# Gathered rows written to memory in one piece per half, statistics included

## The chip, the core and the metric

The kernel runs on one core of one Trainium2 chip. The metric is the device time of one execution in microseconds (us), read as the median of several runs.

## The reference

The input is x of shape (2, 2048, 128): two batches of 2048 tokens with 128 features. It goes through three residual blocks:

```python
x = x + 0.5 * ffn(layernorm(x))
x = x + attention(layernorm(x))
x = x + 0.5 * ffn(layernorm(x))
```

The feed-forward block is a mixture of four experts, of which each token uses one:

```python
idx = argmax(softmax(x @ Wg + bg))
h = gelu(x @ W1[e] + b1[e])          # 128 -> 512
y = h @ W2[e] + b2[e]                # 512 -> 128
out = sum over e of y[e] * onehot(idx)[e]
```

The attention is linear: 32 features elu(.)+1 per token for query and key, a sum k'v over the whole batch, and a normalisation of each token.

## The kernel before

**Tokens are sorted by expert.** A phase is one feed-forward block on one batch; there are four, in the order block one of batch 0, of batch 1, block two of batch 0, of batch 1. Before a phase, the router finds each token's expert and the place of the token in an order sorted by expert, and makes from it a table of row numbers, `src` (written by DVE in `route_src`). In a phase GpSimd (POOL) issues 16 indirect DMAs, `gather`, each of which fetches 128 rows in that order from a tensor in HBM into a tile G. Such a row has `RW` = 144 floats: the 128 features, then the mean, the reciprocal of the deviation (`rstd`), the token's own number and padding, so that whatever is known of the token travels with it. The tensors are `rows0` for the first block and `rows1` for the second, one for each batch.

**The visits.** A phase is worked off in V = 19 visits v, 16 tiles plus three borders between experts. For a visit, DVE normalises the gathered tile (`norm`, xn from G), TensorE (PE) turns it over (`turn_in`), ACT copies it to `hT_in`, PE multiplies by W1 (`up`), ACT applies Gelu, PE multiplies by W2 (`down`), and DVE adds the result to the tile in place (`finish`). PE does `up` three visits ahead of `down`. The weights of a visit with their biases are a slab, which SP copies within SBUF from the tile W1 five visits ahead (`copy_slab`). The sequence of each engine's instructions is written out by hand, in loops over v; semaphores alone tie the engines together.

**The front.** Before the first visit SP loads x of batch 0 in four pieces (`load_x`, into X0_0) and of batch 1 in two (X0_1), then W1 and b2. DVE computes bn_stats on each row of x, and the mean into `MR0`; POOL computes rstd (`pow_front`, a power, one instruction for each half of a batch); PE turns x over and multiplies by the gate weights, with ACT copying between the two (`front_copy`); DVE then routes. PE runs products of no use (`busy`) where it would otherwise wait, the longest being 24 of them ahead of tile 0.

**How rows0 is written before.** Features and statistics go apart. SP stores the features of a half as 8 strips of 512 bytes a partition (`store_x`), as soon as x has landed: for batch 0 ahead of the four loads of W2, for batch 1 at v = 2 and 4 of the first phase. The statistics, strips of 64 bytes, come from `MR0` (`store_stats`): ACT issues them for batch 0, and SP for batch 1 at v = 7 and 8. The first gather of a batch waits for all four stores (64 counts), as well as for `src`.

**What follows from program order.** A wait on SP holds up the slab copies behind it; a wait on ACT holds up the `front_copy` of the next group; a wait on POOL holds up all later gathers. POOL starts with two `pow_front`, a small product `place_tiles`, then eight gathers, then one for each visit, with the two `pow_front` of batch 1 at v = 3 and 4.

Of the kernel before, what the change touches and what calls it, by code (L numbers as in the profile page):

```python
# [16 lines left out]
def need(eng, stage, j):  # L17
    if j >= 0:
        eng.wait_ge(stage.sem, j + 1)
# [15 lines left out]
def build(nc, x, wq, wk, wv, proj, w1, b1, w2, b2, wg, bg, out):  # L35
    f32, bf16, i32 = mybir.dt.float32, mybir.dt.bfloat16, mybir.dt.int32
    ALU, ACT, AX = mybir.AluOpType, mybir.ActivationFunctionType, mybir.AxisListType

    P = 128
    B, L, D = x.shape  # L40
    NE, _, F = w1.shape
    R = proj.shape[1]
    NC = F // P
    T = L // P
# [5 lines left out]
    RW = D + 16  # L50
# [5 lines left out]
    XN = (4, 2)  # L56
# [7 lines left out]
    rows0_v = [r.rearrange("(p t) c -> p t c", t=T) for r in rows0]  # L64
    rows1_v = [r.rearrange("(p t) c -> p t c", t=T) for r in rows1]

    with ExitStack() as ctx:
        def sb(name, shape, dt=f32):
            return ctx.enter_context(nc.sbuf_tensor(name, shape, dt))

        def several(name, shape, n, dt=f32):
            return [sb(f"{name}{i}", shape, dt) for i in range(n)]

        def sem(name):
            return ctx.enter_context(nc.semaphore(name))

        def stages(prefix, names):
            return {n: Stage(sem(f"s_{prefix}_{n}")) for n in names.split()}
# [32 lines left out]
        same = sb("same", [P, P])  # L111
        warm, rest = sb("warm", [P, 1]), sb("rest", [P, 4 * P])

        X0 = several("X0_", [P, T, D], B)
        ST0 = several("ST0_", [P, T, 6], B)
        MR0 = several("MR0_", [P, T, RW - D], B)
        VE0 = several("VE0_", [P, T], B)
        ra, rb_, rc, rd, re = (sb(n, [P, T]) for n in ("ra", "rb", "rc", "rd", "re"))

# [52 lines left out]
        s_x = [[sem(f"s_x{b}_{i}") for i in range(XN[b])] for b in range(B)]  # L172
        s_rows0 = [sem(f"s_rows0_{b}") for b in range(B)]
        s_rows1 = [sem(f"s_rows1_{b}") for b in range(B)]
        s_const, s_constd, s_same = sem("s_const"), sem("s_constd"), sem("s_same")
        s_fold, s_foldd, s_warm, s_av, s_mean = sem("s_fold"), sem("s_foldd"), sem("s_warm"), sem("s_av"), sem("s_mean")
        s_slab = [sem(f"s_slab{k}") for k in range(NSLAB)]
        s_gather = [[sem(f"s_gather{b}_{t}") for t in range(T)] for b in range(B)]
        s_scatter, s_issued = sem("s_scatter"), sem("s_issued")
        s_dve = sem("s_dve")  # L180
        ln0 = stages("ln0", "ve rstd")
# [9 lines left out]
        def ph_of(f, b):  # L191
            return 2 * f + b
# [88 lines left out]
                return {10: range(4, 7), 11: (7,), 13: (8, 9)}.get(v, ())  # L281
            return range(v - NE, T) if v == V - 1 else (v - NE,) if v >= NE else ()

        def store_stats(eng, b, h):
            lo, hi = h * T // 2, (h + 1) * T // 2
            need(eng, ln0["rstd"], 2 * b + h)
            eng.dma_start(rows0_v[b][:, lo:hi, D:RW], MR0[b][:, lo:hi, :]).then_inc(s_rows0[b], 16)


        @block.sync  # L290
        def _(eng):
            H = T // 2
            w1_v = W1[:, :].rearrange("p (e k) -> p e k", e=NE)
            w2_v = W2[:, :].rearrange("p (c e d) -> p e c d", e=NE, d=D)

            def load_x(b, i):
                n = T // XN[b]
                eng.dma_start(X0[b][:, i * n:(i + 1) * n, :], x_b[b][:, i * n:(i + 1) * n, :]).then_inc(s_x[b][i], 16)

            def load_w2(e):  # L300
                eng.dma_start(w2_v[:, e, :, :], w2[e, :, :].rearrange("(c p) d -> p c d", p=P)).then_inc(s_w["w2"], 16)

            def store_x(b, h):
                for i in range(h * XN[b] // 2, (h + 1) * XN[b] // 2):
                    eng.wait_ge(s_x[b][i], 16)
                eng.dma_start(rows0_v[b][:, h * H:(h + 1) * H, 0:D], X0[b][:, h * H:(h + 1) * H, :]).then_inc(s_rows0[b], 16)

            for i in range(XN[0]):
                load_x(0, i)
            load_x(1, 0)  # L310
            load_x(1, 1)
            eng.dma_start(w1_v[:, :, 0:F], w1.rearrange("e d f -> d e f")).then_inc(s_w["w1"], 16)
            eng.dma_start(w1_v[:, :, F + NC:SW], b2.unsqueeze(0).to_broadcast([P, NE, D])).then_inc(s_w["b2"], 16)
            store_x(0, 0)
            store_x(0, 1)
            for e in range(NE):
                load_w2(e)

            def store_rows1(b, g):
                need(eng, lb["x2"], b * NG + g)  # L320
                need(eng, lb["rstd"], b * NG + g)
                need(eng, rt["src"], b)
                eng.dma_start(rows1_v[b][:, g * GS:(g + 1) * GS, :].rearrange("p t c -> p (t c)"),
                              G0[b][:, g * GS * RW:(g + 1) * GS * RW]).then_inc(s_rows1[b], 16)

            offs = {}

            def copy_slab(s):
                ph, v = divmod(s, V)
                if v % CHUNK == (s == 1):  # L330
                    need(eng, rt["visit"], ph)
                    v -= v % CHUNK
                    offs.update({ph * V + v + i: e for i, e in enumerate(loaded(eng, v_slab, ph, v, SW))})
                k = s % NSLAB
                need(eng, ffn["hT"], s - NSLAB)
                need_res(eng, s - NSLAB)
                eng.dma_start(slab[k][:, :], W1[:, bass.ds(offs[s], SW)]).then_inc(s_slab[k], 16)

            eng.wait_ge(s_w["w1"], 16)
            eng.wait_ge(s_w["b2"], 16)  # L340
            eng.wait_ge(s_foldd, 4)

            eng.dma_start(slab[0][:, :], W1[:, 0:SW]).then_inc(s_slab[0], 16)
            for s in range(1, SLAB_LEAD):
                if s > 1:
                    need(eng, ffn["norm"], s - 1)
                copy_slab(s)
            for s in range(2 * B * V):
                ph, v = divmod(s, V)
                if s + SLAB_LEAD < 2 * B * V:  # L350
                    copy_slab(s + SLAB_LEAD)
                if ph == 0 and v in (2, 4):
                    store_x(1, v // 2 - 1)
                if ph == 0 and v in (7, 8):
                    store_stats(eng, 1, v - 7)
                if ph in (1, 2) and 6 <= v < 6 + NG:
                    store_rows1(ph - 1, v - 6)

# [2 lines left out]
        def _(eng):  # L361
# [7 lines left out]
            for b in range(B):  # L369
                eng.memset(MR0[b][:, :, :], 0.0).then_inc(s_const, 1)  # L370
            eng.wait_ge(s_const, 7)
            for b in range(B):
                eng.iota(MR0[b][:, :, 2].bitcast(i32), pattern=[[1, T]], base=b * L, channel_multiplier=T).then_inc(s_const, 1)
            eng.affine_select(out=blocks[:, :], in_=blocks[:, :], compare_op=ALU.is_ge, fill=0.0, base=0,
# [18 lines left out]
            def pow_front(b, h):  # L393
                lo, hi = h * T // 2, (h + 1) * T // 2
                need(eng, ln0["ve"], 2 * b + h)
                ln0["rstd"].done(eng.tensor_tensor(MR0[b][:, lo:hi, 1], VE0[b][:, lo:hi], neghalf[:, lo:hi], ALU.pow))  # L396

# [20 lines left out]
            def gather(f, b, t, second=False, columns=4 * P):  # L418

                if second:  # L420
                    next(count)
                else:
                    rested(columns)
                if t == 0:
                    need(eng, rt["src"], ph_of(f, b))
                    if f == 0:
                        eng.wait_ge(s_rows0[b], 64)
                    else:
                        eng.wait_ge(s_rows1[b], 16 * NG)
                eng.indirect_dma_start(out=row(f, b, t, 0, RW), out_offset=None, in_=(rows0, rows1)[f][b],  # L430
                                       in_offset=bass.IndirectOffsetOnAxis(ap=src[f][b][:, t:t + 1], axis=0),
                                       engine_sem=issued.sem)\
                   .then_inc(s_gather[b][t], 16)
# [98 lines left out]
        def _(eng):  # L532
# [17 lines left out]
            def front_stats(b, lo, hi):  # L550
                eng.wait_ge(s_x[b][lo * XN[b] // T], 16)
                for t in range(lo, hi):
                    did(eng.bn_stats(ST0[b][:, t, :], X0[b][:, t, :]), t == hi - 1)

# [340 lines left out]
        def _(eng):  # L895
# [4 lines left out]
            def front_turn(k):  # L900
# [3 lines left out]
                for i in range(GS):  # L904
                    n = eng.transpose(U[k % 2][:, i * P:(i + 1) * P], X0[b][:, g * GS + i, :], ident[:, :])
                fr["xT"].done(n)
# [213 lines left out]
        def _(eng):  # L1120
# [10 lines left out]
            def front_copy(k):  # L1131
                need(eng, fr["xT"], k)
                need(eng, fr["mm"], k - 2)
                fr["xTs"].done(eng.activation(xTs[k % 2][:, :], U[k % 2][:, :], ACT.Copy))

            def copy_in(ph, j):
                first, n = GROUPS[j]
                need(eng, ffn["xT"], group(ph, j))
                ffn["xTs"].done(eng.activation(hT_in[ph % 2][:, first * P:(first + n) * P], TR[:, 0:n * P], ACT.Copy))  # L1139
# [47 lines left out]

            for k in range(NG):
                front_copy(k)
            front_copy(NG)  # L1190
            front_copy(NG + 1)
            store_stats(eng, 0, 0)
            store_stats(eng, 0, 1)
            hots(0, NG - 1)
            place_lanes(0)
            front_copy(NG + 2)
# [8 lines left out]
            for s in range(2 * B * V):  # L1205
                ph, v = divmod(s, V)
# [54 lines left out]
```

## Time and profile before

| | |
|---|---|
| median of 3 runs (lowest to highest) | 236.23 us (235.95 to 236.77) |
| profiled execution: time, span | 237.53 us, 235.8 us |
| PE busy | 207.2 us (88%) |
| DVE busy | 159.4 us (68%) |
| ACT busy | 126.9 us (54%) |
| POOL busy | 160.2 us (68%) |
| mean granted clock of TensorE | 0.969 |

The span is the time from the first to the last instruction on the core; the profiled execution's own time has 1.73 us around it. The busy time of PE contains the filler products. An engine's idle time counts only where something that ends the kernel waits for it, so the stages have to be read one by one.

### The profile page before, as it was taken

How to read it: one execution, taken by the hardware profiler on the slowest of the kernel's cores; microseconds unless marked ns; L12 is line 12 of the kernel's file. 1: busy time of each engine (PE TensorE's matmuls, PEld its weight loads, DVE VectorE, ACT ScalarE, POOL GpSimd, SP SyncE). 2: the span in 40 equal slices, each digit the busy share in tenths (PEclk: the TensorE clock that was granted, in tenths of full speed). 3: DMA queues.
4: the chain of work that ended last, by engine and by line, in shares of the span. 5: the costliest groups of instructions: out<-in, count | busy, mean ns of one | idle time of the engine just before them, and what ended most of it. 6: DMA issues, size and time to landing. Idle time of an engine off the chain costs nothing. (4 is left out here: it accounts for less than half of the span.)

```text
span 235.8 us, 6375 instructions
## 1 busy us (share of the span) xinstructions
PE 207.2 (88%) x1786; PEld 195.7 (83%) x1786; DVE 159.4 (68%) x641; ACT 126.9 (54%) x406; POOL 160.2 (68%) x225
## 2 busy tenths in 40 slices
PE   8989996996997999999969998999959899999900
PEld 7879996896997988889969897779959899999900
DVE  3699463579688989698887879788776545553400
ACT  1415055567554586635675676825565567765500
POOL 7221888882728687147138888756878888788775
PEclk9999999998899999999999999999979999999985
DMA  4999259982534462326703852517721976662111
GB/s 103 372 321 254 96 199 351 314 212 83 185 110 167 154 215 69 130 106 237 277 0 116 300 206 83 165 61 281 269 79 42 329 274 222 222 221 103 45 56 45
DMA packets 28454, 41.69 MB, mean 177 GB/s; under 512 B 7795, under 2 KB 14851, under 8 KB 28422
## 3 DMA queue, kind: packets, MB, share of 16 engines
q1 hardware_dynamic: 22368, 34.11, 40.5%
q0 software_dynamic: 3072, 6.82, 11.1%
q10 hardware_dynamic: 2982, 0.36, 1.0%
q8 instruction: 16, 0.26, 0.5%
q14 instruction: 16, 0.13, 0.2%
HBM read 9.41 MB, written 6.82 MB: 69 GB/s over the span
## 5 line engine op out<-in xcount | busy, mean ns | idle before, releaser
L1145 ACT ACTIVATE hT<-U,slab 128x128 f32<-128x128 f32 x304 | 86.7, 370 | 56.4 <-PE U L966 56.3
L966 PE MATMUL U<-hT_in,slab 128*128 (+1 forms) x608 | 82.8, 280 | 1.5 <-ACT hT_in L1139 1.3
L977 PE MATMUL DN<-W,hT 128*128 (+1 forms) x608 | 83.7, 282 | 0.2 <-issue 0.2
L966 PEld LDWEIGHTS U<-hT_in,slab 128*128 128x128 f32 x608 | 74.8, 194 | 2.7 <-issue 2.4
L977 PEld LDWEIGHTS DN<-W,hT 128*128 128x128 f32 x608 | 75.4, 195 | 1.4 <-issue 1.2
L430 POOL DMA_INDIRECT G<-rows,src x64 | 62.5, 977 | 15.2 <-issue 10.2
L729 DVE SCALAR_TENSOR_TENSOR G<-DN,mask,G 128x128 f32 (+1 forms) x76 | 26.4, 348 | 27.3 <-PE DN L977 24.6
L416 POOL MEMSET rest<- 128x512 f32 (+1 forms) x78 | 35.4, 454 | 6.3 <-DVE G L729 0.7
L442 POOL DMA_INDIRECT out_dram<-G x32 | 31.6, 988 | 7.3 <-issue 6.3
L705 DVE TENSOR_SCALAR xn<-G 128x128 f32<-128x128 f32 x64 | 23.7, 389 | 9.3 <-DMA G<-rows,src 9.0
L717 DVE SCALAR_TENSOR_TENSOR G<-slab,mask,G 128x128 f32 (+1 forms) x60 | 21.2, 353 | 6.7 <-DVE G L729 4.0
L1139 ACT ACTIVATE hT_in<-TR 128x128 f32<-128x128 f32 (+1 forms) x44 | 14.4, 327 | 17.8 <-PE TR L957 17.4
L957 PE MATMUL TR<-ident,xn 128*128 128x128 f32 x64 | 14.6, 280 | 7.5 <-DVE xn L705 6.3
L401 POOL TENSOR_TENSOR RS<-VE,neghalf 128x4 f32<-128x4 f32 x8 | 8.5, 1062 | 12.9 <-DVE VE L741 12.8
L406 POOL TENSOR_TENSOR G<-VE,neghalf 128x4 f32<-128x4 f32 x8 | 8.3, 1043 | 12.8 <-DVE VE L799 12.6
L957 PEld LDWEIGHTS TR<-ident,xn 128*128 128x128 f32 x64 | 8.3, 142 | 8.8 <-DVE xn L705 7.2
L898 PE MATMUL DN<-mean_w 128*128 128x128 f32 x104 | 14.6, 300 | 1.1 <-POOL mean_w L362 1.1
L898 PEld LDWEIGHTS DN<-mean_w 128*128 128x128 f32 x104 | 13.9, 215 | 1.1 <-POOL mean_w L362 1.1
L467 POOL TENSOR_TENSOR AV<-A,lane_f 128x256 bf16<-128x256 bf16 x4 | 3.3, 828 | 12.5 <-DVE A L651 6.9
L396 POOL TENSOR_TENSOR MR<-VE,neghalf 128x8 f32<-128x8 f32 x4 | 6.7, 1679 | 5.7 <-DVE VE L564 5.2
L734 DVE BATCH_NORM_STATS2 ST<-G 128x6 f32<-128x128 f32 x32 | 8.8, 287 | 1.6 <-issue 1.4
L656 DVE TENSOR_TENSOR SL<-slot_i,lane_b 128x512 bf16<-128x512 int32 x12 | 8.8, 784 | 0.0
(159 smaller groups left out, 219.7 us busy)
## 6 DMA issues: line engine op xcount, KB each, us to landing
slab<-W SPq DMA_DIRECT2D x76, 322.0 KB, 3.1
rows<-G SPq DMA_DIRECT2D x8, 288.0 KB, 2.1
rows<-X SPq DMA_DIRECT2D x4, 512.0 KB, 9.5
X<-in_L_attn_x_dram SPq DMA_DIRECT2D x4, 256.0 KB, 6.7
X<-in_L_attn_x_dram SPq DMA_DIRECT2D x2, 512.0 KB, 8.8
W<-in_L_ffn_W_dram SPq DMA_DIRECT2D x1, 1024.0 KB, 11.5
W<-in_L_ffn_W_dram SPq DMA_DIRECT2D x4, 256.0 KB, 6.0
G<-rows,src POOLq DMA_INDIRECT x64, 3.2
```

The costliest lines, as they stand in the source:

```text
L416: eng.memset(rest[:, 0:columns], 0.0)
L430: eng.indirect_dma_start(out=row(f, b, t, 0, RW), out_offset=None, in_=(rows0, rows1)[f][b], in_offset=bass.IndirectOffsetOnAxis(ap=src[f] ...
L442: eng.indirect_dma_start(out=out_rows, out_offset=bass.IndirectOffsetOnAxis(ap=index, axis=0), in_=row(1, b, t), in_offset=None, engine_se ...
L705: ffn["norm"].done(eng.tensor_scalar(xn[k % NXN][:, :], row(f, b, t), row(f, b, t, D, 1), row(f, b, t, D + 1, 1), ALU.subtract, ALU.mult))
L717: ffn["res"].done(eng.scalar_tensor_tensor(out=r, in0=slab[s % NSLAB][:, F + NC:SW], scalar=mask[f][b][:, v:v + 1], in1=r, op0=ALU.mult, o ...
L729: ffn["out"].done(eng.scalar_tensor_tensor(out=r, in0=DN[s % 2][:, 0:D], scalar=mask[f][b][:, v:v + 1], in1=r, op0=ALU.mult, op1=ALU.add))
L898: eng.matmul(DN[0][:, 0:P], mean_w[:, :], mean_w[:, :], start=True, stop=True)
L957: last = eng.transpose(TR[:, i * P:(i + 1) * P], xn[k % NXN][:, :], ident[:, :])
L966: i = eng.matmul(U[s % 3][:, c * P:(c + 1) * P], slab[s % NSLAB][:, c * P:(c + 1) * P], hT_in[ph % 2][:, bass.ds(v * P - expert_at[s], P)] ...
L977: i = eng.matmul(DN[s % 2][:, 0:D], hT[s % NHT][:, c * P:(c + 1) * P], W2[:, bass.ds(expert_at[s] + c * NE * D, D)], start=(c == 0 and not ...
L1139: ffn["xTs"].done(eng.activation(hT_in[ph % 2][:, first * P:(first + n) * P], TR[:, 0:n * P], ACT.Copy))
L1145: i = eng.activation(hT[s % NHT][:, c * P:(c + 1) * P], U[s % 3][:, c * P:(c + 1) * P], ACT.Gelu, bias=slab[s % NSLAB][:, F + c:F + c + 1])
```

## The change

A tile `XR` of 16 rows of 144 floats a partition takes the place of the statistics' tile, for each batch; the statistics are its last 16 columns. Batch 1 is loaded straight into the first 128 columns of `XR1`. Batch 0 is still loaded into a tile of its own, and ACT copies it to `XR0` in four instructions, behind `front_copy(3)`. One DMA a half then stores features and statistics together, 4608 contiguous bytes a partition on both sides. In batch 0 it waits for the copies and for rstd; the second half goes between the second and third load of W2. In batch 1 the stores stand at v = 5 and 6. ACT issues none. The first gather of a batch waits for two stores (32 counts).

```diff
-        X0 = several("X0_", [P, T, D], B)
+        XR = several("XR", [P, T, RW], B)
+        X0 = [sb("X0", [P, T, D])[:, :, :], XR[1][:, :, 0:D]]
...
-        MR0 = several("MR0_", [P, T, RW - D], B)
+        MR0 = [r[:, :, D:RW] for r in XR]
...
+            def store_rows0(b, h):
+                need(eng, ln0["rstd"], 2 * b + h)
+                if b == 0:
+                    eng.wait_ge(s_copied, (h + 1) * XN[0] // 2)
+                else:
+                    eng.wait_ge(s_x[b][h], 16)
+                eng.dma_start(rows0_v[b][:, h * H:(h + 1) * H, :].rearrange("p t c -> p (t c)"),
+                              XR[b][:, h * H:(h + 1) * H, :].rearrange("p t c -> p (t c)")).then_inc(s_rows0[b], 16)
...
-            store_x(0, 0)
-            store_x(0, 1)
-            for e in range(NE):
-                load_w2(e)
+            store_rows0(0, 0)
+            load_w2(0)
+            load_w2(1)
+            store_rows0(0, 1)
+            load_w2(2)
+            load_w2(3)
...
-                if ph == 0 and v in (2, 4):
-                    store_x(1, v // 2 - 1)
-                if ph == 0 and v in (7, 8):
-                    store_stats(eng, 1, v - 7)
+                if ph == 0 and v in (5, 6):
+                    store_rows0(1, v - 5)
...
-                        eng.wait_ge(s_rows0[b], 64)
+                        eng.wait_ge(s_rows0[b], 32)
...
+            def copy_rows(i):
+                lo, hi = i * T // XN[0], (i + 1) * T // XN[0]
+                eng.wait_ge(s_x[0][i], 16)
+                eng.activation(XR[0][:, lo:hi, 0:D], X0[0][:, lo:hi, :], ACT.Copy).then_inc(s_copied, 1)
...
             for k in range(NG):
                 front_copy(k)
+            for i in range(XN[0]):
+                copy_rows(i)
             front_copy(NG)
             front_copy(NG + 1)
-            store_stats(eng, 0, 0)
-            store_stats(eng, 0, 1)
```

On SP's queue, at the start of the program, these stood before (output and input of each DMA, and the semaphores it waits for; s_x0 and s_x1 tell of the landing of x, and W is W1 or W2 by its shape, 128x4x512 being W1 and 128x4x128 either b2 or W2):

```order
L298 DMA X_0<-in_L_attn_x_dram 128x512 x4
L298 DMA X_1<-in_L_attn_x_dram 128x1024 x2
L312 DMA W<-in_L_ffn_W_dram 128x4x512
L313 DMA W<-in_L_ffn_b_dram 128x4x128
L306 DMA rows_0<-X_0 128x8x128 [waits s_x0_1,s_x0_0]
L306 DMA rows_0<-X_0 128x8x128 [waits s_x0_3,s_x0_2]
L301 DMA W<-in_L_ffn_W_dram 128x4x128 x4
```

And these stand there now:

```order
L297 DMA X<-in_L_attn_x_dram 128x512 x4
L297 DMA XR<-in_L_attn_x_dram 128x8x128 x2
L315 DMA W<-in_L_ffn_W_dram 128x4x512
L316 DMA W<-in_L_ffn_b_dram 128x4x128
L308 DMA rows_0<-XR 128x1152 [waits s_copied,s_ln0_rstd]
L300 DMA W<-in_L_ffn_W_dram 128x4x128 x2
L308 DMA rows_0<-XR 128x1152 [waits s_copied,s_ln0_rstd]
L300 DMA W<-in_L_ffn_W_dram 128x4x128 x2
```

The stores have become one run of 1152 floats a partition, wait for more, and are apart; the load of batch 1 has become eight runs of 128 floats a partition, where it was one of 1024.

On SP's queue, in the first phase, this stretch stood before (ISA sets the address of a slab copy; the TENSOR_LOAD reads the table of visits). It begins with the second store of features of batch 1, at v = 4, and ends with the store of statistics at v = 7:

```order
L306 DMA rows_1<-X_1 128x8x128 [waits s_x1_1]
L337 ISA [waits s_ffn_res,s_ffn_hT]
L337 DMA slab<-W 128x644
L337 ISA [waits s_ffn_res,s_ffn_hT]
L337 DMA slab<-W 128x644
L264 TENSOR_LOAD v_slab_0 [waits s_rt_visit]
L337 ISA [waits s_ffn_res,s_ffn_hT]
L337 DMA slab<-W 128x644
L287 DMA rows_1<-MR_1 128x8x16 [waits s_ln0_rstd]
```

Now the two slab copies of v = 4 and 5 stand ahead of the first store of batch 1, and one more between the stores:

```order
L342 ISA [waits s_ffn_res,s_ffn_hT]
L342 DMA slab<-W 128x644
L342 ISA [waits s_ffn_res,s_ffn_hT]
L342 DMA slab<-W 128x644
L308 DMA rows_1<-XR 128x1152 [waits s_x1_0,s_ln0_rstd]
L342 ISA [waits s_ffn_res,s_ffn_hT]
L342 DMA slab<-W 128x644
L308 DMA rows_1<-XR 128x1152 [waits s_x1_1,s_ln0_rstd]
```

What was stored at v = 2 and 4 has moved behind the slab copy of v = 5, and each store there now waits for POOL's rstd.

## Rows read from the trace of the kernel before

**Rows 1.** The page of the profiled execution: DMA busy tenths in 40 slices of 5.9 us:

```profile
DMA  4999259982534462326703852517721976662111
```

**Rows 2.** Busy time by stage: stretch, its length, each engine, PEclk, DMA share, GB/s:

```profile
23.00:41.00 18.00, 16.20 (x140) 15.67 (x139) 8.47 (x40) 6.91 (x26) 14.78 (x20) 1.00 0.63 209
51.00:62.00 11.00, 8.88 (x74) 8.16 (x73) 10.17 (x42) 6.31 (x21) 5.49 (x8) 0.84 0.47 144
62.00:75.00 13.00, 12.34 (x111) 12.14 (x109) 9.52 (x39) 7.79 (x27) 7.39 (x11) 1.00 0.45 155
186.00:224.00 38.00, 38.00 (x341) 38.00 (x342) 17.74 (x55) 25.26 (x90) 31.50 (x45) 1.00 0.56 194
```

**Rows 3.** Timeline of PE: start, us, engine, line, tiles, idle before:

```profile
23.25 5.55 PE L898 MATMUL DN<-mean_w 128*128 128x128 f32 x48
41.51 0.44 PE L957 MATMUL TR<-ident,xn 128*128 128x128 f32 x2 [2.25 <-DVE xn L705]
56.34 0.44 PE L957 MATMUL TR<-ident,xn 128*128 128x128 f32 x2 [1.91 <-DVE xn L705]
```

**Rows 4.** Timeline of DVE:

```profile
22.33 0.18 DVE L691 TENSOR_SCALAR src<-tok 128x16 int32<-128x16 f32 x1
41.04 0.42 DVE L705 TENSOR_SCALAR xn<-G 128x128 f32<-128x128 f32 x1 [2.48 <-DMA G<-rows,src]
49.19 0.35 DVE L705 TENSOR_SCALAR xn<-G 128x128 f32<-128x128 f32 x1 [0.75 <-DMA G<-rows,src]
60.86 0.17 DVE L691 TENSOR_SCALAR src<-tok 128x16 int32<-128x16 f32 x1
```

**Rows 5.** Timeline of POOL:

```profile
12.35 1.65 POOL L396 TENSOR_TENSOR MR<-VE,neghalf 128x8 f32<-128x8 f32 x1 [0.93 <-DVE VE L564]
24.10 1.20 POOL L430 DMA_INDIRECT G<-rows,src  x1 [4.30 <-DMA rows<-MR]
42.95 1.70 POOL L396 TENSOR_TENSOR MR<-VE,neghalf 128x8 f32<-128x8 f32 x1 [0.45 <-DVE G L729]
44.84 1.01 POOL L430 DMA_INDIRECT G<-rows,src  x1 [0.18 <-issue]
61.32 1.04 POOL L430 DMA_INDIRECT G<-rows,src  x1 [0.55 <-DVE src L691]
```

**Rows 6.** Landings, from issue: b2 (L313); gathers (L430) from 24 and 36 us; statistics (L287):

```profile
L313 SPq DMA_DIRECT2D W<-in_L_ffn_b_dram x1: 947/947/947, 4.3 to 4.3; - x1
DMA to landing us min/median/max: 11.6/11.6/11.6
...
DMA to landing us min/median/max: 2.8/3.3/3.5
...
L430 POOL DMA_INDIRECT G<-rows,src x4: 950/950/977, 36.4 to 41.5; - x4
DMA to landing us min/median/max: 4.0/4.9/5.3
...
L287 ACTq DMA_DIRECT2D rows<-MR x2: 395/510/624, 15.6 to 16.1; - x2
DMA to landing us min/median/max: 4.9/6.0/7.2
```

**Rows 7.** SP's DMA queue: timeline of the loads of W2; instructions of L306 from 34 us:

```profile
13.23 5.26 SPq L301 DMA_DIRECT2D W<-in_L_ffn_W_dram  x4
...
L306 SPq DMA_DIRECT2D rows<-X x2: 601/760/920, 35.8 to 39.6; - x2
```

**Rows 8.** DMA in 8 to 11, 15 to 18 and 19 to 22 us:

```profile
DMA packets 693, 1.21 MB, mean 402 GB/s; under 512 B 186, under 2 KB 358, under 8 KB 693
...
DMA packets 1760, 0.86 MB, mean 286 GB/s; under 512 B 112, under 2 KB 1759, under 8 KB 1759
...
q10 hardware_dynamic: 1409, 0.09, 32.2%
```

**Rows 9.** Timeline of ACT:

```profile
15.19 0.60 ACT L1134 ACTIVATE xTs<-U 128x512 f32<-128x512 f32 x1 [3.49 <-PE U L905]
```

More of the change, by code:

```diff
@@ L176, in build @@
         s_fold, s_foldd, s_warm, s_av, s_mean = sem("s_fold"), sem("s_foldd"), sem("s_warm"), sem("s_av"), sem("s_mean")
+        s_copied = sem("s_copied")
         s_slab = [sem(f"s_slab{k}") for k in range(NSLAB)]
@@ L282, in stats_of @@
             return range(v - NE, T) if v == V - 1 else (v - NE,) if v >= NE else ()
[L284 to L287, printed above, removed]
         @block.sync
@@ L301, in load_w2 @@
                 eng.dma_start(w2_v[:, e, :, :], w2[e, :, :].rearrange("(c p) d -> p c d", p=P)).then_inc(s_w["w2"], 16)
[L303 to L306, printed above, removed]
+            def store_rows0(b, h):
[6 more added lines that the diff above has]
+                              XR[b][:, h * H:(h + 1) * H, :].rearrange("p t c -> p (t c)")).then_inc(s_rows0[b], 16)
             for i in range(XN[0]):
```

## The prediction, made before the changed kernel ran

> **What bounds the kernel now.** I read the page's slices of DMA activity first: the queues are full in the front (up to about 24 us) and again around 36 to 46 us, and the change acts in just these two places [rows 1]. Then the busy times by stage: late in the kernel PE has no idle time (38.00 of 38.00 us), so there nothing but its own work counts, while in 23 to 41 us it lacks 1.8 of 18, and in 51 to 62 us it is DVE that is full, 10.17 of 11 [rows 2]. The timelines say what those gaps are. PE waits 2.25 us ahead of 41.51 for xn, and DVE, which makes xn, waits 2.48 us until 41.04 for a gather [rows 3, 4]. DVE waits again, 0.75 us, ahead of 49.19, and from there it works through the router of the next phase without a stop, so that PE waits 1.91 us for it ahead of 56.34 [rows 3, 4]. Third, POOL: its first gather starts at 24.10, and was released by the statistics' store, though `src` was ready at 22.33 + 0.18 = 22.51 [rows 4, 5]. The last statistics were issued at 16.1 and took 7.2 us to land, at 23.3 [rows 6].
>
> The lateness of the first gather is not yet a lateness of the kernel. PE's filler runs from 23.25 to 28.80, and covers tile 0 [rows 3]. The gathers follow each other at POOL's own pace, though, so an early start helps whichever tile PE first has to wait for, and that is tile 7, whose gather was issued at 36.4 [rows 6].
>
> **The change part by part.**
>
> *The load of batch 1* is now in strips of 512 bytes. The mean rate in 8 to 11 us, large strips, is 402 GB/s; in 15 to 18 us, nearly all strips of 512 bytes, it is 286 [rows 8]. 1.05 MB take 2.6 us at the one and 3.7 at the other: 1.1 us more, in front of W1 and b2 on the same queue. The Trainium skill's page "DMA: Bandwidth & Descriptors", in its section "Specifications", puts the least transfer for full rate at 512 bytes; by that the 1.1 us would be nothing. The two rates above disagree with it here, and I go by them.
>
> *The stores of batch 0.* Before, 1.05 MB at 286 GB/s, 3.7 us, plus 64-byte strips: in 19 to 22 us 1409 packets of ACT's queue, most of the 2048, took 32.2% of three us, so some 1.4 us in all [rows 8]. Now 1.18 MB in strips of 4608 bytes, at 402 GB/s 2.9 us. That is 2.2 us less traffic against 1.1 more. When is the second half in? b2 was issued at 4.3 and landed 11.6 us later, at 15.9 [rows 6]; with the slower load 17.0. Behind it are the first half (0.59 MB, 1.5 us), two loads of W2 (0.52 MB at 286, 1.8 us) and the second half, 1.5 us: 21.8. The issue is no limit: rstd of half 1 is ready at 12.35 + 1.65 = 14.0 [rows 5]. ACT is idle from 15.19 - 3.49 = 11.70 on, waiting for PE, and four copies at the price of its copy of the same size at 15.19, 0.60 each, end at 14.1, hidden with 1.1 to spare [rows 9]. At 0.87 each they would still be. SP was ready for W2 at 13.23 before [rows 7], and now issues the first half at about 12.9, so the queue, full until 17, does not run dry. DVE's and POOL's work on the statistics keeps its count; only the stride of its elements changes, at no cost that I can see.
>
> *The first gather* then waits for `src` at 22.51, and not for the rows. Its start: a gather released by `src` later on starts 61.32 - (60.86 + 0.17) = 0.29 us behind it, while the first one started 24.10 - 23.3 = 0.8 behind the rows' landing [rows 4, 5]. So between 22.80 and 23.3, a gain of 0.8 to 1.3 us; I take 1.2, since the rows' wait is passed before `src` comes, as in the later gather.
>
> *The stores of batch 1* leave v = 2 and 4 (issued at 35.8 and 39.6 [rows 7]). Gathers up to 36 us landed in 2.8 to 3.5 us; the four from 36.4 to 41.5, beside those stores, in 4.0 to 5.3 [rows 6]. Gather 7 now starts at 36.4 - 1.2 = 35.2; with 3.5 us it has landed at 38.7, and its xn, 0.3 to 0.4 us of DVE, is ready at about 39.1. PE was free at 41.51 - 2.25 = 39.26. The whole 2.25 us goes.
>
> *What is late next.* POOL loses its 0.45 us of idle time ahead of 42.95, so its power of batch 1 comes 1.2 + 0.45 less 0.1, about 1.55 us earlier, and gather 11 starts at 44.84 - 1.55 = 43.3 [rows 5]. The first store of batch 1 is released by that same power, at 44.65 - 1.55 = 43.1, so it moves next to gather 11. With 3.4 us (as undisturbed) xn of tile 11 begins at 46.7, with 4.3 us (the disturbed end being 4.0 to 5.3) at 47.6; DVE is free for it at 49.19 - 0.75 - 2.25 = 46.2. Before it was 49.19: a lead of 1.6 to 2.5. The store (0.59 MB) occupies the queues for 1.5 us only, and so I take 2.2. From there DVE and then PE are full [rows 2], and everything that follows is released by events, none by a time: the lead stays.
>
> *SP's new waits* for rstd at v = 5 and 6 have the slab copies of v = 6 and 7 behind them. These are made five visits ahead; the second wait ends with POOL's second power, behind gather 11, about 44.84 + 1.01 + 1.70 - 1.55 = 46.0 [rows 5], and the slab behind it, of visit 12, is used by PE after 56.34. This costs nothing until that wait lasts some 7 us longer.
>
> **Sum.** 237.53 of the profiled execution lies 1.3 us above the median of the runs, and the gain applies to both. 237.53 - 2.2 = 235.3 for such an execution, and 236.23 - 2.2 = 234.0 for the median.
>
> **Rivals.**
>
> *A, the gathers stay slow.* If 4.0 to 5.3 us come from the burst of slab copies at that place and not from the stores, gather 7 lands at 35.2 + 4.7 = 39.9 (4.7, since it was in by 41.04 from 36.4), PE resumes at 40.3, and only the 1.2 us are won: 235.0. For it: slab copies fill the same queue. Against it: the seven gathers up to 36 us, the last of which ran beside slab copies too, took 3.5 at most [rows 6]. The Trainium skill, page "DMA: Bandwidth & Descriptors", section "Queues, rings and completion order", has each DMA engine take turns between queues packet by packet, so that a gather should not wait for a whole store; that speaks for A, and the landings of rows 6 against. The same time comes out if the stores, moved next to gathers 11 and 12, hold those up by a further 1 us. Chance 0.16.
>
> *B, no change.* In 51 to 62 us the granted clock was 0.84, so part of that stretch ran at 1.2 GHz and not at 2.4, and PE lost 0.16 x 11 = 1.8 us there, beneath a DVE that was full anyway [rows 2]. If with other gaps the low stretch comes in 62 to 75 us, where PE is busy 12.34 of 13, most of it counts, and the gain shrinks to 0.4 to 0.7: 235.7. Chance, with anything else that takes the lead back, 0.12.
>
> *C, slower.* The second half of batch 0 stands behind the load of batch 1, W1, b2, the first half and half of W2, with itself 1.05 + 1.05 + 0.26 + 0.59 + 0.52 + 0.59 = 4.1 MB from about 8 us on. If strips of 512 bytes on two queues together brought it down to 230 GB/s, four fifths of the 286, it would land at 25.7, and the first gather start at 26.5, 2.4 us late. The filler ends at 28.80, and xn of tile 0 could be there at about 24.10 + 2.8 + 0.7 = 27.6, so 1.2 us are covered and PE is 1.2 behind; gather 7, from 38.8, gives its xn at 42.6, 1.1 later than PE had it: 237.3. It decides from a landing at about 25 on. Against it stands that the traffic in all has become smaller. Chance 0.06.
>
> **How the numbers follow.** My forecast, 233.0 to 234.9, has 0.66, A 0.16, B 0.12, C 0.06. The prediction is 234.0. To leave out no more than two in ten, the range reaches over A to the edge of B: 232.9 to 235.7. The low end is the upper bound of both terms: 0.1 more at the first gather and no wait at all for tile 11, 3.0 off (0.75 + 2.25), with 0.3 of scatter. About 0.3%, 0.7 us, is what a measurement can tell from no change; faster than that are the forecast and most of A, 0.80; within it B, 0.13; slower 0.07.
>
> **What would show it.** First gather at 22.8 to 23.3, released by `src`; the second store landed before 22.5. No wait of PE ahead of tiles 6 and 7, gathers 7 to 10 landing in under 4 us. xn of tile 11 at 46.6 to 47.6, PE's wait for DVE at about 54. Wrong would be: a first gather that still names rows as its releaser, landings beyond 4 us, a low clock in the stretch in which PE is full, or a wait for a slab.

## The result, and the profile after

The changed kernel takes 234.93 us, the median of 8 runs (233.85 to 236.17); the kernel before 236.24, the median of 8 (235.27 to 237.21). The ratio is 0.9941 [0.9913, 0.9968]: 1.3 us less. The profiled execution took 236.17 us with a span of 234.4; the one of before had 237.53 and 235.8, so 1.4 less there too. The forecast was 2.2 less. The ratios of this document leave disturbed executions out, which is why some are not the quotient of the two medians beside them.

The page of the changed kernel, DMA by slices and in all; before, [rows 1], the page had 28454 packets with 7795 under 512 bytes:

```profile
DMA  4998369682534461336604853517712976662111
DMA packets 22502, 41.69 MB, mean 178 GB/s; under 512 B 3635, under 2 KB 8643, under 8 KB 22470
```

Its busy time by stage, columns as in [rows 2]:

```profile
23.00:41.00 18.00, 17.26 (x151) 16.81 (x150) 9.24 (x42) 7.30 (x28) 15.69 (x21) 1.00 0.61 209
51.00:62.00 11.00, 9.14 (x77) 8.62 (x77) 9.56 (x39) 6.49 (x21) 5.34 (x8) 0.84 0.43 146
```

PE now works 17.26 of the 18 us up to 41, where it worked 16.20. In 51 to 62 us nothing has changed but a small shift; the granted clock is the same 0.84.

Its timeline, SP's queue, ACT, DVE, POOL and PE one after the other:

```profile
3.77 5.42 SPq L315 DMA_DIRECT2D W<-in_L_ffn_W_dram  x1
9.24 0.96 SPq L316 DMA_DIRECT2D W<-in_L_ffn_b_dram  x1
...
12.59 0.34 SPq L308 DMA_DIRECT2D rows<-XR  x1
...
14.56 0.61 SPq L308 DMA_DIRECT2D rows<-XR  x1
...
43.10 0.34 SPq L308 DMA_DIRECT2D rows<-XR  x1
...
11.36 2.18 ACT L1142 ACTIVATE XR<-X 128x512 f32<-128x512 f32 x4
14.95 1.09 ACT L1137 ACTIVATE xTs<-U 128x512 f32<-128x512 f32 x2 [1.42 <-PE U L908]
...
22.06 0.17 DVE L694 TENSOR_SCALAR src<-tok 128x16 int32<-128x16 f32 x1
...
39.03 0.34 DVE L708 TENSOR_SCALAR xn<-G 128x128 f32<-128x128 f32 x1 [1.12 <-DMA G<-rows,src]
...
47.82 0.35 DVE L708 TENSOR_SCALAR xn<-G 128x128 f32<-128x128 f32 x1 [1.86 <-DMA G<-rows,src]
...
23.05 1.20 POOL L433 DMA_INDIRECT G<-rows,src  x1 [3.51 <-DVE src L694]
...
41.38 1.69 POOL L399 TENSOR_TENSOR XR<-VE,neghalf 128x8 f32<-128x8 f32 x1
43.24 1.01 POOL L433 DMA_INDIRECT G<-rows,src  x1 [0.17 <-issue]
...
39.43 0.44 PE L960 MATMUL TR<-ident,xn 128*128 128x128 f32 x2 [0.74 <-DVE xn L708]
...
48.22 0.44 PE L960 MATMUL TR<-ident,xn 128*128 128x128 f32 x2 [0.86 <-DVE xn L708]
...
55.03 0.44 PE L960 MATMUL TR<-ident,xn 128*128 128x128 f32 x2 [1.79 <-DVE xn L708]
```

The landings, from issue: the two stores of batch 0; the gathers issued before 35.5 us; gather 11 alone:

```profile
L308 SPq DMA_DIRECT2D rows<-XR x2: 345/479/613, 12.6 to 14.6; - x2
...
DMA to landing us min/median/max: 5.3/6.4/7.6
...
DMA to landing us min/median/max: 2.6/3.2/3.8
...
DMA to landing us min/median/max: 4.6/4.6/4.6
```

Read against [rows 3] and [rows 4], the place where PE stood still is the same, and shorter: 39.43 with 0.74 of idle time, where it was 41.51 with 2.25. That is 2.08 us won, nearly all of it in two parts: gather 7 was issued 1.13 us earlier (35.22 and not 36.35), mostly because the first one came at 23.05 instead of 24.10 [rows 5], and DVE had it 3.81 us behind its issue (39.03) and not 4.69 (41.04). Then 0.7 us are given back at one place: gather 11, issued at 43.24, 0.14 us behind the first store of batch 1 (43.10), took 4.6 us. PE waits 0.86 us ahead of 48.22, where it had not waited before. The lead at tile 11 is 49.19 - 47.82 = 1.37 us, and the spans differ by as much at the end (1.4). The last result of the first phase starts at 82.21 on DVE, and started at 83.53.

### The profile page after: what moved, and what is told of

It is laid out like the page before. It is cut to its first block and busy times, and to the rows that moved or that the text cites. A ratio compares the mean times of both kernels' runs of the same rounds, so it can differ in the third digit from the quotient of the medians.

```text
span 234.4 us, 6377 instructions
## 1 busy us (share of the span) xinstructions
PE 206.2 (88%) x1786; PEld 194.9 (83%) x1786; DVE 158.9 (68%) x641; ACT 129.1 (55%) x410; POOL 160.3 (68%) x225
## 5 line engine op out<-in xcount | busy, mean ns | idle before, releaser
L433 POOL DMA_INDIRECT G<-rows,src x64 | 62.6, 978 | 14.3 <-issue 10.1
L404 POOL TENSOR_TENSOR RS<-VE,neghalf 128x4 f32<-128x4 f32 x8 | 8.4, 1044 | 12.9 <-DVE VE L744 12.8
L409 POOL TENSOR_TENSOR G<-VE,neghalf 128x4 f32<-128x4 f32 x8 | 8.4, 1044 | 12.8 <-DVE VE L802 12.6
L399 POOL TENSOR_TENSOR XR<-VE,neghalf 128x8 f32<-128x8 f32 x4 | 6.9, 1717 | 5.0 <-DVE VE L567 5.0
```

## The experiments

The kernels were run on three occasions, each with 35 executions of the kernel before beside 12 of every other kernel; one execution of each kernel left a trace. On two of the occasions all kernels, the one before among them, took some 250 us and not 236: the granted clock fell again and again between 170 and 217 us. The busy times of such a kernel in that stretch (here `late_rows`, columns as in [rows 2]):

```profile
170.00:218.00 48.00, 32.03 (x208) 30.08 (x209) 14.23 (x50) 16.48 (x59) 33.68 (x50) 0.75 0.35 116
```

Up to 170 us these traces are like the others, and the readings below are taken there; the times of those two occasions have intervals of 0.4 to 0.5% either way, too wide for a part of this change.

**The parts alone.** `b0_only` packs batch 0 and leaves batch 1 as it was; `b1_only` is the opposite. The cores of the edits, both shown against the changed kernel (what follows from them in tiles and helpers is left out):

```diff
 # b0_only
-                if ph == 0 and v in (5, 6):
-                    store_rows0(1, v - 5)
+                if ph == 0 and v in (2, 4):
+                    store_x(1, v // 2 - 1)
+                if ph == 0 and v in (7, 8):
+                    store_stats(1, v - 7)
...
 # b1_only
-            store_rows0(0, 0)
-            load_w2(0)
-            load_w2(1)
-            store_rows0(0, 1)
-            load_w2(2)
-            load_w2(3)
+            store_x(0, 0)
+            store_x(0, 1)
+            for e in range(NE):
+                load_w2(e)
...
-            for i in range(XN[0]):
-                copy_rows(i)
...
+            store_stats(eng, 0, 0)
+            store_stats(eng, 0, 1)
```

> Batch 0 as in the changed kernel, batch 1 as before (features at v = 2 and 4, statistics at v = 7 and 8, loaded into a tile of its own). Sum of the prediction, first term alone: first gather 1.0 to 1.1 us earlier, gathers 7 to 10 still at 4.0 to 5.3 us beside the stores, PE's stall ahead of tiles 6 and 7 about 1.2 us; 1.0 us under before, a ratio of 0.996. Theory S says the same. Theory P (the packing of batch 0 is all of the gain): a ratio of 0.994, as the whole change.

> Batch 0 as before, batch 1 as in the changed kernel. The first gather is where it was before, about 24.1 us. Theory S: gather 7 lands in 3.5 to 3.9 us, so the stall ahead of tiles 6 and 7 shrinks from 2.25 to about 1.1 us, but gather 11 runs beside the first store at v = 5 and takes about 4.5 us, so that only 0.3 us of it is left: a ratio of 0.998 to 1.000. Theory P: no gain, 1.000. A gain of 1 us or more (0.996 or less) would speak against S.

`b0_only`: 251.06 us beside 250.69, 1.0027 [0.9978, 1.0076]. `b1_only`: 251.22 beside 250.69, 1.0038 [1.0003, 1.0074]. Both were run once more, on another occasion:

> Batch 0 packed, batch 1 as before, once more, for a time that the low clock after 170 us does not blur. By the earlier trace of this kernel, which was 0.9 us ahead of the kernel before at 138 us: a ratio of 0.996. If the packing of batch 0 gave nothing: 1.000.

> Batch 0 as before, batch 1 packed, once more. By the earlier trace, 1.6 us ahead at 138 us with the low stretch of the clock missing before 62 us, which may be 0.8 of it: a ratio of 0.996 to 0.997. Theory S as first written, 0.998 to 1.000.

`b0_again`: 250.51 beside 251.37, 0.9960 [0.9915, 1.0004]. `b1_again`: 251.00 beside 251.37, 0.9958 [0.9917, 0.9998]. The two results of `b1_only` contradict each other, each with an interval that leaves 1 out, so on these occasions the intervals are too narrow to be trusted with 0.4%; the times only say that neither part is worth more than about 1% by itself. The traces say what each does. Timeline of `b0_only`, POOL and DVE:

```profile
22.62 1.20 POOL L441 DMA_INDIRECT G<-rows,src  x1 [3.01 <-DVE src L702]
...
39.93 0.35 DVE L716 TENSOR_SCALAR xn<-G 128x128 f32<-128x128 f32 x1 [2.42 <-DMA G<-rows,src]
```

And of `b1_only`:

```profile
23.83 1.20 POOL L435 DMA_INDIRECT G<-rows,src  x1 [4.10 <-DMA rows<-MR]
...
39.67 0.35 DVE L710 TENSOR_SCALAR xn<-G 128x128 f32<-128x128 f32 x1 [1.46 <-DMA G<-rows,src]
```

The early first gather belongs to batch 0 (22.62, and 22.50 the second time; with batch 1 alone 23.83 and 24.41, still released by the statistics). With batch 0 alone tile 7 comes only 1.1 us earlier and its gather still takes 5.21 us; with batch 1 alone it takes 3.66 and tile 7 comes 1.4 earlier. The second traces have 1.7 us (`b0_again`, gather 4.74) and 0.8 us (`b1_again`, gather 3.71). So the early first gather comes with batch 0 and the quick gather 7 with batch 1, as was expected, and the whole change, 2.0 us earlier at this tile, has both; how much each is worth scatters by more than half a us between executions.

**The stores of batch 1 elsewhere.** `late_rows` is the changed kernel with the stores at v = 8 and 9; `before_x_late` is the kernel before with its feature stores at v = 8 and 9.

```diff
 # late_rows
-                if ph == 0 and v in (5, 6):
-                    store_rows0(1, v - 5)
+                if ph == 0 and v in (8, 9):
+                    store_rows0(1, v - 8)
 # before_x_late
-                if ph == 0 and v in (2, 4):
-                    store_x(1, v // 2 - 1)
+                if ph == 0 and v in (8, 9):
+                    store_x(1, v - 8)
```

> The changed kernel, with the two stores of batch 1 at v = 8 and 9 instead of 5 and 6. Theory S (a store of rows beside a gather holds the gather up by about 1 us): gather 11, which took 4.6 us to land in the changed kernel, takes 3.3 to 3.6 here, DVE's wait of 1.86 us ahead of xn of tile 11 falls below 0.9, and the time is about 1.2 us under the changed kernel, near 233.7 us or a ratio of 0.990. Theory L (gathers 11 and 12 are slow because of slab copies or of the power between them, whatever is stored): the landing stays above 4.2 us, and the time stays at the changed kernel's, a ratio of 0.994. If the later stores delay the first gather of batch 1 (at about 60 us), that gather names rows as its releaser and both are hidden.

> The kernel before, with nothing changed but the two stores of batch 1's features, moved from v = 2 and 4 to v = 8 and 9. Theory S: gathers 7 to 10 land in 3.3 to 3.9 us instead of 4.0 to 5.3, the stall ahead of tiles 6 and 7 falls from 2.25 to about 1.1 us, gather 11 lands in under 3.8, and the kernel gains 1.2 to 1.4 us, a ratio of 0.994 to 0.995, with no packing at all. Theory L (the slab copies hold those gathers up): landings and time as before, 1.000.

`late_rows`: 249.73 beside 250.69, 0.9884 [0.9832, 0.9936]. `before_x_late`: 250.99 beside 250.69, 0.9975 [0.9930, 1.0021]; the interval holds both the 1.000 of theory L and the 0.994 to 0.995 of theory S. Timeline of `before_x_late`, POOL and DVE:

```profile
22.87 1.20 POOL L430 DMA_INDIRECT G<-rows,src  x1 [3.30 <-DVE src L691]
...
39.47 0.73 DVE L705 TENSOR_SCALAR xn<-G 128x128 f32<-128x128 f32 x1 [2.01 <-DMA G<-rows,src]
```

Theory S missed here in part: with no store beside it gather 7, issued at 35.09, still took 4.38 us to its xn (3.3 to 3.9 were expected), and PE waited 1.55 us for it and not 1.1. And two gains of the whole change turn up without any packing: the first gather starts at 22.87, because the statistics had landed by 15.8 + 6.1 = 21.9 in this execution, and the last result of the first phase at 82.03, where the changed kernel had 82.21. Timeline of `late_rows`, DVE and PE:

```profile
46.53 0.44 DVE L708 TENSOR_SCALAR xn<-G 128x128 f32<-128x128 f32 x1 [0.58 <-DMA G<-rows,src]
...
54.08 0.44 PE L960 MATMUL TR<-ident,xn 128*128 128x128 f32 x2 [1.76 <-DVE xn L708]
```

With the stores issued at 45.32 and 47.93, tile 11 comes at 46.53 and PE does not wait for it; its wait for the router stands at 54.08, 0.95 earlier than with the stores at v = 5 and 6. Then the kernel before, the changed one and this one were run together, on the occasion on which the kernel before took 236.55:

> The kernel before, unchanged, for a trace on the same chip as the others of this call. Ratio 1.000. If the last runs' chip is typical of its kind, its first gather starts at 22.9 to 24.1 us, by src or by the statistics; ahead of tiles 6 and 7 PE waits about 2 us, gathers 7 to 10 take over 4 us.

> The changed kernel, unchanged, on the same chip. Ratio 0.994 (between 0.991 and 0.997). Both theories: gather 11 lands in about 4.5 us beside the first store of batch 1.

> The changed kernel with the stores of batch 1 at v = 8 and 9, once more, beside the changed kernel on one chip. Theory S: 0.4 to 0.5% below the changed kernel, a ratio to before of 0.989 to 0.990; xn of tile 11 about 1.2 us earlier than in the changed kernel, gather 11 landing in 3.3 to 3.7 us. If the first measurement of it was scatter, its ratio is 0.994.

`before_again`: 236.99, 0.9989 [0.9955, 1.0022], the measure of how well this tells kernels apart. `after_again`: 235.29, 0.9939 [0.9910, 0.9968], the first result over again, in other executions. `late_again`: 235.02, 0.9922 [0.9892, 0.9951], not told apart from it. In the trace of `after_again` gather 11 was in good time, and in that of `late_again` gather 12 was not. Timeline of `after_again`, DVE:

```profile
46.37 0.35 DVE L708 TENSOR_SCALAR xn<-G 128x128 f32<-128x128 f32 x1 [0.81 <-DMA G<-rows,src]
```

Timeline of `late_again`, DVE and PE, and under it, as the source view of the gathers' line has it for 45.5 to 47 us, the landing of gather 12, issued at 45.86 beside the store at 45.78:

```profile
51.29 0.35 DVE L708 TENSOR_SCALAR xn<-G 128x128 f32<-128x128 f32 x1 [1.72 <-DMA G<-rows,src]
...
55.16 0.44 PE L960 MATMUL TR<-ident,xn 128*128 128x128 f32 x2 [3.44 <-DVE xn L708]
```

```profile
DMA to landing us min/median/max: 5.4/5.4/5.4
```

So a store at v = 8 can have the next gather land late in its turn; in `late_rows`, with the same store 0.6 us ahead of gather 12, DVE did not have to wait for that gather. `late_again` led by 2.92 us at tile 11 (49.19 - 46.27), and its last result of the phase started at 82.26, no earlier than that of the changed kernel (82.21).

**The first gather.** The profile of the changed kernel names `src` as what released it, but 0.82 us lie between the two, where it was 0.29 at a later gather [rows 4, 5]. Two kernels were made to find the rest. `late_warm` is `late_rows` with one more indirect DMA on POOL ahead of the first gather; it fetches a row of wk that nothing reads. `rows_first` is the changed kernel with both stores of batch 0 ahead of the loads of W2.

```diff
 # late_warm
             pow_front(0, 1)
+            next(count)
+            eng.indirect_dma_start(out=first_row[:, :], out_offset=None, in_=wk,
+                                   in_offset=bass.IndirectOffsetOnAxis(ap=exp_no_i[:, 0, 0:1], axis=0),
+                                   engine_sem=issued.sem).then_inc(s_first, 16)
             place_tiles(0)
...
 # rows_first
             store_rows0(0, 0)
-            load_w2(0)
-            load_w2(1)
             store_rows0(0, 1)
-            load_w2(2)
-            load_w2(3)
+            for e in range(NE):
+                load_w2(e)
```

> The last kernel with one more indirect DMA on POOL, of one row of wk into a tile that nothing reads, issued when POOL is idle at about 14 us. Theory F (the first indirect DMA of a program costs extra: it starts 0.8 us behind its release and takes 1.20 us, later ones 0.29 and 0.95 to 1.04): the first real gather starts 0.3 us behind src and takes under 1.1 us, the gathers after it 0.6 to 0.8 us sooner; since gathers 7 to 11 are still waited for by 0.6 to 1.2 us, the time falls by a further 0.3 to 0.6 us, a ratio of 0.987 to 0.988. Rival W (the delay belongs to waiting on src, or to the queue): the first gather still starts 0.8 us behind src, and the time is that of the kernel without it.

> The changed kernel with both stores of batch 0 ahead of all four loads of W2. Theory R (the first gather starts at the later of src + 0.30 us and the last landing of the rows + 0.87 us, and in the changed kernel the second held): the second store lands about 1.8 us earlier, near 20.3 us, and the first gather starts 0.30 us behind src, at 22.5 to 22.7, whatever the run; 0 to 0.5 us earlier than in the changed kernel, a ratio of 0.992 to 0.994. Rival (the place between pieces of W2 has a use of its own: W2 becomes late): down(0) waits for W2 at about 34 us, and the time rises.

`late_warm`: 234.69 beside 236.55, 0.9919 [0.9893, 0.9946], the same as `late_again`. Timeline of `late_warm`, POOL:

```profile
13.90 1.18 POOL L489 DMA_INDIRECT first_row<-in_L_attn_Wk_dram,exp_no_i  x1 [0.18 <-issue]
...
24.10 0.99 POOL L434 DMA_INDIRECT G<-rows,src  x1 [4.13 <-DMA rows<-XR]
```

The first call costs 1.18 to 1.20 us and the next 0.99: being first is worth 0.2 us of the call, and no more. The start did not get earlier, since in this trace the rows landed at 15.5 + 7.8 = 23.3 and held it up to 24.10. Theory F is wrong about the start: the gather was no longer the first call, and still started 0.8 us behind its release, here the rows' landing. `rows_first`: 250.96 beside 251.37, 0.9914 [0.9865, 0.9962]. Landing of its two stores (12.8 to 14.0), then its timeline, POOL:

```profile
DMA to landing us min/median/max: 4.8/5.1/5.4
```

```profile
22.77 1.20 POOL L431 DMA_INDIRECT G<-rows,src  x1 [3.01 <-DVE src L692]
```

With the rows in at 14.0 + 5.4 = 19.4, three us ahead of `src`, the gather starts 0.30 us behind `src` (22.30 + 0.17 = 22.47). And W2, behind both stores, was not missed by PE. Theory R came out.

**Both together.** `first_late10` is `rows_first` with the stores of batch 1 at v = 10 and 11, behind the last gather that PE has to wait for:

```diff
-                if ph == 0 and v in (5, 6):
-                    store_rows0(1, v - 5)
+                if ph == 0 and v in (10, 11):
+                    store_rows0(1, v - 10)
```

> rows_first with the stores of batch 1 at v = 10 and 11 besides. Theory S: at v = 8 they stood beside gather 12, which then took 5.4 us; at v = 10, SP reaches them at about 51 us, behind the last gather that DVE waits for, so gathers 7 to 13 land in 2.5 to 4 us, xn of tile 11 starts at about 46.3 and PE's wait ahead of 54 us is 1.7 us and not 3.4; a ratio of 0.989 to 0.991. Rival: the rows of batch 1 land behind src of the next phase (about 58.5 us), and its first gather waits for them; a ratio of 0.993 or more.

249.00 us beside 251.37, 0.9888 [0.9842, 0.9934], the lowest ratio but one of the twelve runs, and level with `late_rows`. Its timeline, DVE and PE:

```profile
46.35 0.57 DVE L706 TENSOR_SCALAR xn<-G 128x128 f32<-128x128 f32 x1 [0.82 <-DMA G<-rows,src]
...
53.60 0.44 PE L958 MATMUL TR<-ident,xn 128*128 128x128 f32 x2 [2.07 <-DVE xn L706]
```

The wait ahead of 53.60 is PE's only one of over 0.3 us between 33 and 58 us, and the last result of the first phase starts at 80.99, 2.5 us ahead of before. The stores, issued at 50.77 and 56.37, are late enough to hold up the first gather of batch 1, to 60.87 with `src` ready at 58.61, as the rival had it; the ratio of 0.993 or more that went with it did not come. On this occasion its interval and that of `rows_first` (0.9914) overlap, so that the times do not show that the later place is better. Nor do the traces, as this table of all fourteen shows; a star marks those with a granted clock of 1.00 and not 0.84 in 51 to 62 us:

| | first gather starts | last result of the first phase starts |
|---|---|---|
| before; `before_again`* | 24.10; 24.94 | 83.53; 83.25 |
| `before_x_late` | 22.87 | 82.03 |
| `b0_only`; `b0_again`* | 22.62; 22.50 | 82.62; 80.88 |
| `b1_only`*; `b1_again`* | 23.83; 24.41 | 81.87; 82.47 |
| after; `after_again` | 23.05; 22.60 | 82.21; 81.06 |
| `late_rows`; `late_again`; `late_warm` | 22.72; 22.84; 24.10 | 81.16; 82.26; 82.33 |
| `rows_first`; `first_late10` | 22.77; 22.72 | 81.92; 80.99 |

With the clock alike, the two executions of the changed kernel lie 1.2 us apart, which is about as much as lies between it and any variant; one trace of each does not rank them. Every kernel with something of the change is ahead of both traces of the kernel before.

## Why the prediction was right, and where it was off

The sign, the two places and the range held (234.93 in 232.9 to 235.7). The point forecast was 0.9 us too low: 234.93 lies at the upper edge of the main case (233.0 to 234.9) and is the number of rival A (235.0). In the profiled execution the term that was mis-sized is the landing of gather 11 under "What is late next": 3.4 to 4.3 us were allowed, "the store (0.59 MB) occupies the queues for 1.5 us only", and it took 4.6, so that the lead at tile 11 was 1.37 us where 2.2 had been taken. Its issue was as forecast: 43.3, and it was 43.24.

Two sets of numbers speak for the store as the cause. The first is gather 7, from its issue on POOL to the start of its xn on DVE, where DVE waited for it:

| | store issued beside it | us from issue to xn |
|---|---|---|
| before; `b0_only`; `b0_again` | 0.6; 0.05; 0.05 us ahead | 4.69; 5.21; 4.74 |
| `before_again` | 0.2 us behind | 3.80 |
| after; `late_rows`; `late_again`; `late_warm`; `rows_first`; `first_late10`; `b1_only`; `b1_again` | none | 3.81; 3.88; 4.03; 3.79; 4.09; 3.79; 3.66; 3.71 |
| `before_x_late` | none | 4.38 |

The second is gather 11, in the same way:

| | store issued beside it | us from issue to xn |
|---|---|---|
| after; `rows_first`; `b1_only`; `b1_again` | 0.14 to 0.15 us ahead | 4.58; 4.42; 4.48; 4.58 |
| `b0_only`; `b0_again` (statistics of batch 1) | 0.9 to 1.0 us behind | 4.96; 4.66 |
| before; `before_again` (statistics of batch 1) | 1.4 to 1.6 us behind | 4.35; 4.68 |
| `after_again` | 0.15 us ahead | 3.66 |
| `before_x_late` (statistics of batch 1) | 1.1 us behind | at most 3.50 (DVE did not wait) |
| `late_rows`; `late_again`; `first_late10`; `late_warm` | over 2 us behind | 3.56; 3.32; 3.52; 3.81 |

The timeline of `before_again` has, for DVE:

```profile
40.83 0.35 DVE L705 TENSOR_SCALAR xn<-G 128x128 f32<-128x128 f32 x1 [0.33 <-DMA G<-rows,src]
```

Leaving out three exceptions, the value with a store is 0.3 to 1.6 us above all those without in the first table, and 0.5 to 1.6 us in the second. The exceptions are `before_again` in the first (gather issued at 37.03, store at 37.25) and `after_again` and `before_x_late` in the second; two of them are executions of the very kernels that have the delay in another. The gathers between these two tell the same: of gathers 8 to 10, in the traces that give their landing, seven near the features' stores of batch 1 took 4.0 to 5.3 us (before, `before_again`, `b0_again`), and of eight in kernels without a store there seven took 2.9 to 3.6 and one, in `after_again`, 4.5. So a store beside a gather goes with a late landing in most cases and not in all; what decides between them stays open.

Whether this delay is also what the median lacks (1.3 us won and not 2.2) is not shown. The execution of the changed kernel that has the delay is the slowest of its eight (236.17, the median 234.93), and the one without it is the fourth of twelve (235.05, the median 235.29), which does not speak for a delay in the usual execution. And `late_again`, with no store beside gather 11, has a median that could not be told from that of `after_again`. The span of `after_again`, 233.3 us, is 2.5 below that of before and 2.1 below that of `before_again`: so the forecast gain of 2.2 us is reached in single executions, but single executions of one kernel differ by 2 us. Nor do the times say what the packing is worth beside the mere place of the stores of batch 1: the interval of `before_x_late`, which packs nothing, is 0.9930 to 1.0021, and that of the whole change 0.9913 to 0.9968.

Step by step:

- *The load of batch 1* was forecast 1.1 us slower. b2, behind it, landed at 9.24 + 7.2 = 16.4, where it had been 15.9: 0.5. The line of the DMA view on 8 to 11 us, where nearly all strips are now 512 bytes:

```profile
DMA packets 2002, 1.00 MB, mean 335 GB/s; under 512 B 218, under 2 KB 1954, under 8 KB 2002
```

  At 335 GB/s 1.05 MB take 3.1 us, at the 402 of [rows 8] 2.6. The 286 that I used was of a stretch with stores and W2 in it. By the rule of the Trainium skill (page "DMA: Bandwidth & Descriptors", section "Specifications") that 512 bytes are enough for full rate there would have been no loss; the rate in these three us was 327 to 335 GB/s in the nine traces whose kernel loads batch 1 in 512-byte strips, and 400 to 408 in the five others, a sixth less.
- *The stores of batch 0.* Second half in at 14.56 + 7.6 = 22.2, forecast 21.8. ACT's copies ended at 13.54 (forecast 14.1), hidden as said.
- *The first gather* came at 23.05 (forecast 22.8 to 23.3), but not quite for the reason given. The profile names `src`, ready at 22.23; 0.82 us lie between it and the gather. With the rows landed at 22.2 it is 0.9 behind these, near the 0.8 of before [rows 5, 6] and of `late_warm`. So the rows still held it, by about half a us: the step "the rows' wait is passed before `src` comes" failed here, and with the prediction's own 0.8 behind a landing at 22.2 the start is 23.0. `late_again` is alike (`src` ready at 22.04, rows in at 14.3 + 7.7 = 22.0, start at 22.84). In `after_again` and `late_rows`, where the rows landed at 20.9 and 21.0, the gather started 0.30 behind `src`, at 22.60 and 22.72. The 1.05 us won in the profiled execution are therefore what the rows' landing moved, 23.3 to 22.2; it moves by itself as well, since it was 21.9 in `before_x_late`, with the front as before, and 23.3 in `late_warm`, with the packed one. `src` lies between 21.86 and 22.33 in thirteen of the fourteen traces, whatever the kernel.
- *The stall ahead of tile 6 and 7* was forecast to go whole; 0.74 us stayed. Gather 7 took 3.81 and not 3.5 us to its xn, so that PE went on at 39.43 and not by 39.26, 0.2 us later than taken; the other half us of its wait is that it had come free earlier, at 39.43 - 0.74 = 38.69, and cost nothing. In `after_again` and `late_again`, with gathers of 34.68 and 34.92, PE has no wait of over 0.3 us there.
- *SP's waits* cost nothing: the one wait of PE for a slab between 23 and 90 us, over all traces, is of 0.5 us at 33.58 in `b1_again`, ahead of both stores.
- *Rival A* had its main cause wrong as a rule: in the eight traces of the first table with batch 1 packed and no store at that place gather 7 took 3.7 to 4.1 us. Single gathers were late with no store beside them all the same (gather 7 of `before_x_late`, and one issued at 29.61 in `after_again`, which DVE had at 34.73, 5.1 us later), so a store is not the only cause. Its last sentence came true in the profiled execution, where gather 11 beside the store was late; it named 235.0, and the median is 234.93, but as said above that the median has this cause is not shown. The Trainium skill's rule that an engine takes turns between queues packet by packet (same page, section "Queues, rings and completion order") was taken in the prediction to mean that a gather need not wait for a whole store; a gather beside one came 0.3 to 1.6 us later in most traces, so the rule does not keep a gather from being late. The section "Latency and other measured facts" of that page has the access time of HBM rise from 0.2 to 2 us under load; the delays are no larger than that, but no run here tells access time from a queue.
- *Rival B:* the low clock stayed in 51 to 62 us (0.84) in the profiled executions of both kernels. In four traces (`before_again`, `b0_again`, `b1_only`, `b1_again`) it was 1.00 there. *Rival C* would have needed a landing at 25 us; the latest of a store in one piece was 23.3.

## What to carry to other kernels

When a large store is moved off the critical gathers, look where its own release puts it next: here it was released by the same POOL instruction that precedes the next critical gather, and in one execution of two a third of the gain was given back there. Behind the last gather that an engine waits for, a store that nothing needs soon meets none of them, and that costs one number in the schedule; that the kernel gets faster by it was not shown here. And a lead of 2 to 3 us at one tile is only worth what survives the next tile: compare a milestone some visits on (here the last result of the phase) rather than the stall that the change removed, and in more than one execution: here two of one kernel differed by 1.2 us at it.

## What the runs showed of the hardware that was not expected

- The rows' last landing and `src` release the first gather with unlike delays, 0.8 to 0.9 and 0.30 us. Why is open.
- The landing of the second store of batch 0, with two loads of W2 ahead of it and batch 1 packed, took 6.2 us (`after_again`, `late_rows`) or 7.6 to 7.8 (after, `late_again`, `late_warm`), though it was issued at 14.3 to 14.8, in `late_warm` at 15.5. A fetch of instructions, 16 KB, lies in those us in all five traces, at 19 to 20 us in the slow ones and at 20 to 21 in the others; that it delays the store was not shown.
- The issue of a load can hold up its engine for microseconds. W1's issue took SP 0.67 us before and 5.42 after, when batch 1's load ahead of it had eight times as many strips; over all traces it is 0.5 to 0.7 us in the five with large strips and 5.2 to 5.6 in the nine with small ones. SP had nothing else to do.
- The clock in the front can be low by itself. Busy time by stage of `before_again` in 16 to 23 us, where all others have 1.00:

```profile
16.00:23.00 7.00, 7.00 (x37) 7.00 (x35) 5.40 (x23) 3.54 (x9) 1.00 (x1) 0.52 1.15 273
```

  PE was busy all 7 us and did half the instructions (37 against 70 in the profiled execution of before); `src` came at 24.47 instead of 22.33, and the first gather at 24.94.
